# First attention: a mask, two film operands and a norm moved between VectorE, ScalarE and GpSimd

## The reference, cut to what matters

```python
x = x + _L0_xattn_ref(_layernorm(x, axis=-1), ctx_768, ...)
...
    Q = (x_text @ Wq).reshape(Bb, Tt, H, DH)
    K = (x_vision @ Wk).reshape(Bb, Gg, H, DH)
    scores = jnp.einsum('bthd,bghd->bhtg', Q, K) / np.sqrt(DH).astype(np.float32)
    topv, topi = jax.lax.top_k(scores, K_TOP)
    probs = jax.nn.softmax(topv, axis=-1)
    attn = jnp.zeros_like(scores).at[bi, hi, ti, topi].set(probs)
    attn_mean = attn.mean(axis=1)
    c_t = jnp.einsum('btg,bgd->btd', attn_mean, V)
    x = layernorm(x_text, g_norm_in, b_norm_in)
    scale_in, shift_in = jnp.split(c_t @ W_film_in + b_film_in, 2, axis=-1)
    x = x * (1.0 + mod_gate * scale_in) + mod_gate * shift_in
    y = s4d(x, log_dt, A_re, A_im, C_re, C_im, D_skip)
    ...
def s4d(x, log_dt, A_re, A_im, C_re, C_im, D_skip):
    ...
    K = 2.0 * jnp.einsum('dn,dnl->dl', dC, powers).real
    Kf = jnp.fft.rfft(K, n=n, axis=-1)
    xf = jnp.fft.rfft(x, n=n, axis=1)
    y = jnp.fft.irfft(xf * Kf.T[None], n=n, axis=1)[:, :L]
    return y + x * D_skip
```

## Time and profile before

| what | value |
|---|---|
| median of three runs | 293.9 us (293.81 to 296.36) |
| profiled execution | 295.63 us, its span 293.7 us |
| busy share of the span | PE 80%, DVE 61%, ACT 52%, POOL 19% |
| first group's masks begin | 58.69 us |
| last copy behind the values (L803) begins | 94.71 us |

### The profile page before, as it was taken

How to read it: one execution, slowest core, us unless ns; L and a number is a source line. 1 busy time by engine, 2 the same in 40 slices (tenths; PEclk the granted TensorE clock), 3 DMA queues, 4 the chain that set the end, 5 groups by cost and what they waited for, 6 DMA issues and landing times.

```text
span 293.7 us, 5241 instructions
## 1 busy us (share of the span) xinstructions
PE 235.0 (80%) x2047; PEld 144.7 (49%) x2071; DVE 180.3 (61%) x463; ACT 153.5 (52%) x250; POOL 55.4 (19%) x87
## 2 busy tenths in 40 slices
PE   1899398659699887798887898988988988877684
PEld 0343132448687442435646765665665655643223
DVE  3289999699992425324364586777766864035553
ACT  2686976479263287453146665565555554802021
POOL 3899589401200001000022000000000000000120
PEclk9999779768599998769999999999999999988979
DMA  6999100200008700000399999989999844600000
GB/s 206 265 340 276 68 1 0 74 2 0 0 2 321 289 35 0 0 0 3 55 106 121 104 135 121 105 113 112 108 109 104 99 55 154 279 0 0 2 0 4
DMA packets 5389, 27.67 MB, mean 94 GB/s; under 512 B 1995, under 2 KB 2188, under 8 KB 3735
## 3 DMA queue, kind: packets, MB, share of 16 engines
q1 hardware_dynamic: 5365, 27.34, 47.7%
HBM read 17.66 MB, written 0.03 MB: 60 GB/s over the span
## 4 chain that ended last, share of the span: by engine, by line
PE 32%; DVE 9%; issue 5%; ACT 4%; POOL 2%; DVEq 0%; POOLq 0%; ACTq 0%
PE B L1046 18%; PE A L1046 13%; DVE mx L938 4%; ACT probs L623 1%; PE B L1363 1%; ACT mid L614 1%; DVE moe_w L935 1%; POOL rstd L359 1%; ACT moe_w L605 0%; ACT L623 0%; POOL ctxn L440 0%; POOL ctxn L442 0%; POOL probs L437 0%; ACT scores L553 0%; DVE late L1015 0%
## 5 line engine op out<-in xcount | busy, mean ns | idle before, releaser
L938 DVE TENSOR_REDUCE mx<-B 128x1 f32<-128x512 f32 (+1 forms) x104 | 65.1, 656 | 26.2 <-PE B L1046 22.0
L623 ACT ACTIVATE probs<-A 128x896 f32<-128x896 f32 x56 | 51.3, 918 | 37.1 <-PE A L1046 36.8
L359 POOL TENSOR_TENSOR rstd<-ve,mhalf 64x1 f32<-64x1 f32 x10 | 5.5, 549 | 208.1 <-DVE ve L661 178.4
L1046 PE MATMUL B<-probs,scores 128*32 128x128 f32 x736 | 34.0, 280 | 4.9 <-ACT mid L614 3.5
L1046 PE MATMUL A<-ctxT,qq 98*128 98x512 f32 (+1 forms) x52 | 27.3, 689 | 5.9 <-ACT scores L472 5.4
L1046 PEld LDWEIGHTS B<-probs,scores 128*32 128x32 f32 x736 | 19.2, 109 | 11.4 <-ACT probs L623 6.6
L1046 PE MATMUL B<-scores,moe_w 128*128 128x512 bf16 (+2 forms) x93 | 21.4, 334 | 1.7 <-issue 1.0
L1046 PEld LDWEIGHTS A<-ctxT,qq 98*128 98x128 f32 x52 | 11.4, 229 | 22.4 <-issue 11.5
L705 DVE MAX8 mid<-scores 128x8 f32<-128x128 f32 x98 | 19.5, 281 | 4.4 <-ACT scores L472 4.3
L1046 PE MATMUL A<-moe_w 112*128 112x128 bf16 (+2 forms) x146 | 19.8, 281 | 0.8 <-DVE moe_w L935 0.7
L788 DVE SCALAR_TENSOR_TENSOR probs<-scores,top,probs 128x512 f32<-128x512 f32 (+1 forms) x26 | 17.6, 720 | 0.0
(11 more groups left out here) (366 smaller groups left out, 383.2 us busy)
## 6 DMA issues: line engine op xcount, KB each, us to landing
ctxT<-scores SPq DMA_DIRECT2D x20, 132.0 KB, 4.6
ctxn<-in_ctxn SPq DMA_DIRECT2D x1, 2352.0 KB, 13.8
moe_w<-in_moe_w SPq DMA_DIRECT2D x1, 2304.0 KB, 8.6
ctxn<-in_moe_w SPq DMA_DIRECT2D x1, 2304.0 KB, 8.6
scores<-in_e_gu SPq DMA_DIRECT2D x1, 2048.0 KB, 7.7
ctxT<-in_ctxT SPq DMA_DIRECT2D x3, 588.0 KB
ctxT<-k_early SPq DMA_DIRECT2D x24, 64.0 KB, 4.2
blob_m<-in_blob_m SPq DMA_DIRECT2D x1, 1467.0 KB, 14.4
```

Source lines behind the costliest of these rows:

```text
L359: nc.gpsimd.tensor_tensor(rstd[:, :], ve[:, :], mhalf[0:T, :], ALU.pow).then_inc(S["rstd_ready"], 1)
L623: A_(probs[:, (n % RING) * 1024:(n % RING) * 1024 + w], A[:, 2 * (n % 2):2 * (n % 2) + 2, :].rearrange("p a b -> p (a b)")[:, 0:w], ACT.Ex ...
L938: V.tensor_reduce(mx[:, m, t:t + 1], bank[:, 0:SB0[t][1]], AX_X, ALU.max).then_inc(S["max_used"], 1)
L1046: return mm(out_, lhsT, rhs, start=start, stop=stop)
```

## The change

- On VectorE the norm is split into `norm_stats` and `norm_apply`. The second norm's statistics now stand behind the copy `x0T`, its apply into `xin` (without gain and shift) behind the masked queries. On GpSimd `rsqrt(2)` moves up, behind the three operations of exponents and turns.
- The mask of `m1` moves: ScalarE copies the two banks into `m1raw` behind the exponentials of group 0, GpSimd multiplies them by the mask. The first four spectrum products move from behind group 0 to behind group 2.
- The film weights are scaled on ScalarE, behind the exponentials of group 2. The film row is made on GpSimd by two operations, and so are gain and shift of `xin`. They stand ahead of `x0b` and the diagonals.

```diff
-SPECTRUM_AT = {0: (0, 4), 3: (4, 6), 4: (6, 8), 5: (8, 10), 6: (10, 12), 7: (12, 14), 8: (14, 16)}
+SPECTRUM_AT = {2: (0, 4), 3: (4, 6), 4: (6, 8), 5: (8, 10), 6: (10, 12), 7: (12, 14), 8: (14, 16)}
...
+        m1raw, = carve(late[:, 8 * D:], P, (2, BANK))
...
             link(nc.gpsimd.tensor_scalar(stt_[:, :], sth[:, :], 1.0 / (2.0 * np.pi), 0.0, ALU.mult, ALU.add))
+            rsqrt(2)
...
             tt(s4q[:, :, :].rearrange("p d l -> p l d"), turns[:, 16:24, :], mags[:, 8:16, :], ALU.mult).then_inc(S["s4_pq"], 1)
-            rsqrt(2)
+            for q in range(2):
+                pool.wait_ge(S["m1_sb"], q + 1)
+                tt(m1[:, 4 * q:4 * q + 4, :].rearrange("p g (d b) -> p (g d) b", b=RB),
+                   m1raw[:, q, :].rearrange("p (g d b) -> p (g d) b", g=4, b=RB),
+                   W["mask_h1"].unsqueeze(1).unsqueeze(3).to_broadcast([P, 4, H1, RB])
+                   .rearrange("p g d b -> p g d b"), ALU.mult).then_inc(S["m1_ready"], 1)
 
             pool.wait_ge(S["ld_m"], 16)
+            pool.wait_ge(S["ld_rows"], 16 * len(ROWS))
+            pool.wait_ge(S["const_ready"], 2)
+            link(ts(W["film_b"], W["film_b"], W["gate"][0:1, :], 0.0, ALU.mult, ALU.add))
+            link(tt(xin[:, :], xin[:, :], W["g_in"], ALU.mult))
+            tt(W["film_1"], W["film_b"], W["film_1"], ALU.add).then_inc(S["film_row"], 1)
+            tt(xin[:, :], xin[:, :], W["b_in"], ALU.add).then_inc(S["film_row"], 1)
             tt(x0b[:, :], W["x"], W["b_out"], ALU.add).then_inc(S["pool_const"], 1)
...
+                if b == 0:
+                    act.wait_ge(S["m1_ps"], 1)
+                    for q in range(2):
+                        A_(m1raw[:, q, :], A[:, q, :], ACT.Copy).then_inc(S["m1_sb"], 1)
+                if b == 2:
+                    act.wait_ge(S["wcf_ps"], 1)
+                    A_(wcf[:, :], A[0:DC, 2, :], ACT.Copy, scale=W["gate"][0:DC, :]).then_inc(S["wcf_sb"], 1)
...
             V.tensor_copy(x0T[:, :], B[0][:, 0:T]).then_inc(S["tokT_sb"], 1)
+            norm_stats(x0[:, :])
             dve.wait_ge(S["q0_ps"], 1)
...
+            norm_apply(xin[:, :], x0[:, :], S["const_ready"])
             dve.wait_ge(S["qq0_ps"], 1)
...
-            dve.wait_ge(S["m1_ps"], 1)
-            for q in range(2):
-
-                V.tensor_tensor(m1[:, 4 * q:4 * q + 4, :].rearrange("p g (d b) -> p (g d) b", b=RB),
-                                A[:, q, :].rearrange("p (g d b) -> p (g d) b", g=4, b=RB),
-                                W["mask_h1"].unsqueeze(1).unsqueeze(3).to_broadcast([P, 4, H1, RB])
-                                .rearrange("p g d b -> p g d b"), ALU.mult).then_inc(S["m1_sb"], 1)
...
-                if b == 4:
-
-                    dve.wait_ge(S["wcf_ps"], 1)
-                    V.tensor_scalar(wcf[:, :], A[0:DC, 2, :], W["gate"][0:DC, :], None, ALU.mult).then_inc(S["wcf_sb"], 1)
-                    dve.wait_ge(S["ld_rows"], 16 * len(ROWS))
-                    V.scalar_tensor_tensor(W["film_1"], W["film_b"], W["gate"][0:1, :], W["film_1"],
-                                           ALU.mult, ALU.add).then_inc(S["film_row"], 1)
-
-                    scaled_norm(xin[:, :], nt[:, :], x0[:, :], W["g_in"], W["b_in"])
...
             dve.wait_ge(S["film_ps"], 1)
+            dve.wait_ge(S["film_row"], 2)
...
-            pe.wait_ge(S["const_ready"], 2)
+            pe.wait_ge(S["const_ready"], 3)
...
-                    pe.wait_ge(S["m1_sb"], 2)
+                    pe.wait_ge(S["m1_ready"], 2)
```

More of the change, by code:

```diff
@@ L103 @@
 rep_ready flag_ps topk_final e_ready w_ready attnT_ps attnT_sb
-dt_ready s4_theta s4_turns s4_sin s4_mag s4_pq m1_ps m1_sb kf_ps kf_sb
+dt_ready s4_theta s4_turns s4_sin s4_mag s4_pq m1_ps m1_sb m1_ready kf_ps kf_sb
 s4_z s4_cs s4_inv s4_gain
@@ L656, in link, with norm_stats @@
                 dve.wait_ge(S["vec_chain"], chain[0])
-            def layernorm(dst, src, signal=None, meanwhile=None):
+            def norm_stats(src):
                 link(V.bn_stats(st[:, :], src))
@@ L662, in layernorm, with norm_apply @@
                 norm[0] += 1
-                if meanwhile:
-                    meanwhile()
+            def norm_apply(dst, src, signal=None):
                 dve.wait_ge(S["rstd_ready"], norm[0])
@@ L670, in layernorm @@
                     link(ins)
+            def layernorm(dst, src, signal=None):
+                norm_stats(src)
+                norm_apply(dst, src, signal)
             def scaled_norm(dst, part, src, g, b):
```

## The result

The changed kernel took 297.44 us in the median of 20 runs, against 294.40 for the kernel before in 20 runs beside it; the ratio is 1.0092 with a 95% interval of 1.0052 to 1.0133. In this measurement it is slower by about 2.7 us (1.5 to 3.9). The forecast was 2.0 more. The ratios here leave disturbed runs out, so they can't be worked out from the medians beside them; single executions of both kernels spread over 8 us and more. Two later measurements of the same two kernels, given under the experiments, found no slowdown in this ratio. The plain mean of every execution on record is 297.98 us for the changed kernel (45 executions) and 295.93 for the kernel before (110), about 2 apart.

The account below looks back on a forecast made before the run. Bound by GpSimd's chain, then VectorE, then TensorE: 4.56 us off VectorE against 1.83 for the root and 3.85 at the port; TensorE's longer run ends 2.0 late, so 293.9 becomes 295.9 us, range 291.8 to 298.6.

Parts of the forecast that it names:

- What bounds the kernel: Around the first attention: GpSimd's chain up to 54.6 us, VectorE from 58.69 to about 76, TensorE from 76.28 on.
- a sign of being wrong: TensorE at group 2: prediction wrong if its clock rises earlier than 5 us after that group.
- The early root: Second square root ahead of L373 on GpSimd: delays its chain and VectorE's loop by 1.83 us; bounds 0 and 1.83.
- The port: VectorE groups 0 to 2 wait on GpSimd's operations: 3.7 us, plus 0.15 for diagonals; bounds 0.5 and 6.7.
- its three copies: ScalarE's added copies of 512 columns, 0.5 to 0.6 us each, hidden by 0.4 us ahead of VectorE's need.
- 2.0 was forecast: TensorE begins group 2 at 70.8, runs 25.9 us without a gap, ends at 96.7 against 94.68.
- Behind the attention: After the attention nothing differs: film weights, row and the scaled, shifted x are ready early.
- (a): Rival: port costs little in VectorE's groups, 0.3 instead of 3.7 us; 292.5 us, chance 0.18.
- (c): Rival: both port cheap and second root's wait covered on GpSimd; 290.7 us, chance 0.07.
- (b): Rival: second root's wait covered on GpSimd's way, without a gain at the port; 294.1 us, chance 0.10.
- (d): Rival: GpSimd holds VectorE for full durations, row operations 1.04 each; 2.5 to 3 more, 298.6 us, chance 0.15.

Follow-up runs that it names:

- root_late: Changed kernel with the second norm's root back behind GpSimd's five large products and the norm's apply made there too; ratio to the kernel before 0.9848.
- no_mask: Changed kernel without the mask of the spectrum's factors, ScalarE copying straight to m1, so another spectrum; ratio to the kernel before 0.9940.
- norm_front: Kernel before with only the second norm moved to the front; masks, film weights, film row, gain and shift stay on VectorE; ratio 0.9936.
- masks_back: Changed kernel with both masks back on VectorE ahead of group 0 and the first four spectrum products behind group 0; ratio to before 0.9941.
- all_idle: Changed kernel, GpSimd reordered: root, apply, row and gains behind the large products, then masks; x0b and diagonals behind the last group; ratio to before 0.9849.
- pool_first: Changed kernel with GpSimd's film row and the norm's gain and shift ahead of its two masks; ratio to the kernel before 0.9951.
- spare: Kernel before, nothing added on GpSimd: film weights on ScalarE, row in a VectorE wait, second norm's end behind the last group; ratios 0.9845 and 0.9866.

## Why the prediction was right

**What bounds the kernel** held in each of its three stretches. GpSimd's chain sets the first: 1.2 us early on it were 1.4 at the first group, and with the root moved back they were gone (root_late). TensorE's full run sets the end: from its start on group 2 to the mark it was 26.4 us in the changed kernel, 25.8 in its third trace, in root_late and in no_mask, against a forecast of 25.9. The 0.6 between them is group 3, which took 2.85 where the clock rose inside it and 2.24 where it was up before. The forecast took the rise at 5 us after the start of group 2 from one trace, and named an earlier rise as a sign of being wrong. It came 5.8 us after in the first trace and 3.4 in the third (0.66 in the window 73 to 74, group 2 begun at 70.28): the 5 us is no constant.

**The early root** was the right mechanism and 0.45 us too dear. The term was 1.83; VectorE reached its loop 1.37 late (60.06 against 58.69), and 1.42 and 1.70 in the other two traces. The length from statistics to GpSimd's next operation was right (6.13 to 7.57 is 1.44, forecast 1.45), the start was not: the statistics began at 6.13 and not at 6.79. In all three traces of the changed kernel VectorE's first apply took 0.34 where it had taken 0.58 before, because GpSimd's next operation waited for ScalarE and had not yet begun (5.39 in the first, 5.07 before). In norm_front GpSimd began at 4.91, the apply took 0.57, and the delay was 1.70.

**The port** was sized at 3.7 for groups 0 to 2 and 0.15 for the diagonals, 3.85 in all, and measured 3.56. The masks cost 0.75 each, not 0.84. Of the 3.56, 0.22 fell into group 3, and TensorE began group 2 at 69.94 instead of 70.8. The Trainium skill's rule in "SBUF — State Buffer", Who interferes with whom, that the pair is held for the whole instruction, is too strong as a price here: VectorE lost 0.75 of each 1.04, and GpSimd's mask was itself stretched to 1.50. Whether the pair is held for less than the instruction, or the loser does part of its work meanwhile, no run here shows. That both operations contend at all, as the rule says of two SBUF inputs against a GpSimd operation that reads SBUF, the traces bear out.

**ScalarE** hid its three copies, as said: in the changed kernel its exponentials of group 1 were done at 62.5, ahead of VectorE's 62.88.

**TensorE** ended 1.6 us late at the mark where 2.0 was forecast; an earlier start by 0.9 and a run longer by 0.5 make the difference. That the two errors partly cancel is luck.

**Behind the attention** "nothing differs" holds for the work, and the forecast had no term for the clock. In one of three traces of the changed kernel the clock was at its lower level for 10 us of the film stage, at a price of 4.3 us (14.65 against 10.32); masks_back and all_idle show the same stretch at the same price. That this belongs to the change is not shown: the two other traces don't have it, the filling of the short waits decided nothing, and in other traces, one of before among them, the clock fell at other places. Of the changed kernel's 45 executions 22 took 298.5 us or more; of the 110 of before 18 did, and 30 took 296.9 or more, which is the fair line for a kernel whose attention ends 1.6 us earlier. So the changed kernel may meet such stretches more often, or not. Of the measured 2.7 us (1.5 to 3.9) the traces show 1.0 to 1.8 in the attention; the rest lies within the interval and has no shown cause. That the measured difference came within 0.7 of the forecast is in part luck, since the later ratios were 0.9951 and 1.0001.

**The rivals.** (a) and (c) fall with no_mask and pool_first, (b) with root_late, (d) with the 3.56. The whole of the loss could be had back in several ways, each with a mark ahead of that of before: root and order (root_late, 92.83), the same work in another order (all_idle, 93.39), or masks and products left in their old places (masks_back, 93.89).

## What to carry to other kernels

Work moved off a busy engine must be followed on the engine that takes it, both in what now stands behind it in order and in the port that both share: here 4.6 us taken off VectorE cost it 3.6 at the port, and one root of 0.55 us, with the waits around it, delayed a chain of 50 us by 1.2. Look for the waits that are there already: GpSimd's 5 us ahead of the masks, VectorE's 0.8 us ahead of `z0` and 5 us behind the last group took the same work for little: with GpSimd's 5 us filled the first group began 0.7 us later (pool_first), and spare's began 0.8 later than before for 3.4 us saved behind group 4. And where an engine ends the stretch with a backlog, two things count: the moment at which it can begin to work without a gap, and what has been moved into that run.

## What the runs showed of the hardware

VectorE's operations with two SBUF inputs and GpSimd's take turns, one by one: beside an uninterrupted row of VectorE operations of 0.70 to 0.75 us GpSimd's 64x128 operations of 0.45 lasted 0.77 to 0.89 and its 128x512 masks 1.50 where such an operation took 1.04 elsewhere, while VectorE's became as long as 1.75. From 60.9 to 71.6 us each of the two began 10 operations. Both engines lose. And TensorE's clock in a stretch of nearly identical work with short waits, behind the attention, was in 11 of the 14 traces at the upper level and in 3 at the lower for about 10 us, with 14.65 us in all three and 10.26 to 10.32 in the others.
